# Gate inputs kept two at a time, products by C in a ring of two, and a reordered prologue in a Mamba scan kernel

## What is computed

```
xz = x @ win.T; u, z = split(xz)                  # 1024 channels each
u  = silu(causal_conv4(u) + bconv)
dt, B, C = split(u @ wx.T)                        # 32, 16, 16
delta = softplus(dt @ wdt.T + bdt)
h[n]  = exp(delta * A[n]) * h[n] + delta*u*B[n]   # 16 states a channel, a scan over time
y  = sum_n h[n] * C[n] + u * D
y  = (y * silu(z)) @ wout.T
```

## Time and profile before

| what | us |
|---|---|
| median of the runs | 7417.18 |
| the profiled execution | 7414.95 |
| its span, first to last instruction | 7413.2 |
| PE busy in it | 6753.6 (91%) |
| VectorE busy | 6890.9 (93%) |
| ScalarE busy | 6151.4 (83%) |
| GpSimd busy | 6961.1 (94%) |

### The profile page before, as it was taken

One profiled execution on the slowest core, in us unless ns is written; L12 is line 12 of the kernel. 1 busy time (PEld: TensorE's weight loads), 2 busy tenths in 40 slices (PEclk: granted clock), 3 DMA queues, 4 the chain that ended last, 5 costly groups with the idle time before them and its releaser, 6 DMA issues. The chain is left out here.

```text
span 7413.2 us, 108939 instructions
## 1 busy us (share of the span) xinstructions
PE 6753.6 (91%) x32598; PEld 4030.3 (54%) x32598; DVE 6890.9 (93%) x9252; ACT 6151.4 (83%) x13132; POOL 6961.1 (94%) x3766
## 2 busy tenths in 40 slices
PE   8999999999999998899999899999999999999889
PEld 4555555555555555555555555555555555555455
DVE  6999999999999999999999999999999999999766
ACT  5888888888888888888888888888888888888645
POOL 5999999999999999999999999999999999999678
PEclk9999999999999999999999999999999999999999
DMA  4454444445444444544444454454444544444555
GB/s 163 131 159 138 125 143 140 140 137 157 133 126 141 135 133 128 152 136 116 144 139 133 128 146 140 110 147 138 133 128 143 152 109 144 133 137 129 164 184 171
DMA packets 581024, 1034.51 MB, mean 140 GB/s; under 512 B 100512, under 2 KB 213408, under 8 KB 572256
## 3 DMA queue, kind: packets, MB, share of 16 engines
q1 hardware_dynamic: 576288, 1025.56, 46.6%
q10 hardware_dynamic: 4160, 2.10, 0.1%
HBM read 901.13 MB, written 126.30 MB: 139 GB/s over the span
## 5 line engine op out<-in xcount | busy, mean ns | idle before, releaser
L513 POOL TENSOR_TENSOR dBu<-Bb,du 128x1024 f32<-128x1024 f32 x2048 | 4796.7, 2365 | 2.5 <-DMA Bb<-bc_scratch 2.5
L652 ACT ACTIVATE scans<-delta,A 128x512 f32<-128x512 f32 x4096 | 2744.3, 696 | 233.4 <-DVE hC L1151 223.4
L1135 DVE TENSOR_TENSOR_SCAN scans<-scans,state,dBu 128x512 f32<-128x512 f32 x2016 | 2535.2, 1278 | 226.0 <-ACT scans L652 223.9
L1135 DVE TENSOR_TENSOR_SCAN dBu<-scans,state,dBu 128x512 f32<-128x512 f32 x1568 | 1956.5, 1260 | 7.4 <-ACT scans L652 7.4
L883 PE MATMUL yT<-ident,hC 128*128 128x128 f32 x9216 | 1389.6, 281 | 274.4 <-DVE hC L1151 272.3
L1151 DVE TENSOR_TENSOR hC<-scans,Cb 128x512 f32<-128x512 f32 x2304 | 1553.2, 678 | 2.9 <-PE yT L883 2.8
L525 POOL TENSOR_TENSOR hR<-dBu,Cb 128x512 f32<-128x512 f32 x1024 | 1306.3, 1276 | 216.3 <-DVE dBu L1135 216.0
L883 PEld LDWEIGHTS yT<-ident,hC 128*128 128x128 f32 x9216 | 1077.0, 144 | 568.4 <-DVE hC L1151 345.5
L599 ACT ACTIVATE turned<-bg,CT 128x128 f32<-128x128 f32 x3072 | 877.1, 370 | 246.2 <-PE bg L860 245.6
L876 PE MATMUL bg<-u,comb 128*128 128x512 f32 x2048 | 963.8, 597 | 50.9 <-ACT pre L612 50.0
L834 PE MATMUL bg<-hT,win_z 128*128 128x512 f32 x2048 | 977.7, 600 | 0.0
(11 more groups left out here) (147 smaller groups left out, 7970.2 us busy)
## 6 DMA issues: line engine op xcount, KB each, us to landing
comb<-pre_scratch SPq DMA_DIRECT2D x1024, 256.0 KB, 4.5
Bb<-bc_scratch SPq DMA_DIRECT2D x264, 512.0 KB, 7.0
Cb<-bc_scratch SPq DMA_DIRECT2D x264, 512.0 KB, 7.1
win_u<-in_win SPq DMA_DIRECT2D x264, 256.0 KB, 4.6
win_z<-in_win SPq DMA_DIRECT2D x257, 256.0 KB, 2.7
pre_scratch<-pre SPq DMA_DIRECT2D x256, 256.0 KB, 3.6
comb<-comb_scratch SPq DMA_DIRECT2D x64, 1024.0 KB, 8.2
part_scratch<-pre SPq DMA_DIRECT2D x128, 256.0 KB, 2.0
```

What stands on the lines that cost most here:

```text
L513: pool.tensor_tensor(dBu[:, ring(g, q)], Bb[:, 2 * q:2 * q + 2, :], du[:, j % 2, :].unsqueeze(1).broadcast_to([P, 2, T]), ALU.mult).then_i ...
L652: act.activation(place(n)[:], delta[:, j % 2, :], ACT.Exp, scale=A[:, i // CH_DIR, j * N + n:j * N + n + 1]).then_inc(dA_made, 1)
L1135: nc.vector.tensor_tensor_scan(to, place(n)[:], dBu[:, ring(g, q), k, :], state[:, c:c + 1] if i % CH_SEQ else 0.0, ALU.mult, ALU.add).the ...
```

## The change

- `z` gets two places, `z[:, tile % 2]`. `take_z` then waits only for the gate of the tile before the last one.
- Z1 moves from positions 9, 10 to 4, 5; Z6 from 49, 50 to 45, 46; Z7 from 58, 59 (bank 0) to 50, 51 (bank 1). The visits at p = 15 and 63 go. The one at 7 does the z of tiles 0 and 1, the one at 53 that of tiles 6 and 7 beside the u pair. Z1 is now taken at p = 7, Z6 at 48, Z7 at 53.
- The parts of O0 to O3 are spread anew: O0 (2, 3, 3, 4, 5, 6, 6, 7), O1 8 to 11, O2 12 to 15, O3 16 to 19. O0 is taken at p = 8 where it was 6, O1 at 12 (11), O2 at 16 (15), O3 at 20 as before.
- D7 moves to bank 0, C7 to bank 1, and the late part of the output matrix to p = 53, after Z7 in bank 1.
- The products `hR` get two places where they had four, so GpSimd's product of state 7 waits for TensorE's add of state 3, and that of state 11 for the add of state 4.
- Work for chunks 32 and 33 is left out (`made_in`), with its loads and waits.
- The prologue: `wmod` comes in four pieces, each with a semaphore, and the modulation matmuls loop over k outside. The skip diagonals are made and stored before the first normalization. The stores of `wtap` and the loads of `wgain`, `wproj` and `wout` are issued by ScalarE between its silu steps. `wgain` lies in `Cb[:, 8:12]`.

```diff
-HC, HR = 4, NA
+HC, HR = 4, 2
 GENERAL = [
-    ("D1", (0,), 0), ("Z0", (1, 2), 1), ("O0", (2, 2, 3, 3, 4, 4, 5, 5), 0), ("O1", (6, 6, 7, 7, 9, 9, 10, 10), 0),
-    ("D2", (7,), 1), ("Z1", (9, 10), 1), ("O2", (11, 11, 12, 12, 13, 13, 14, 14), 0), ("D3", (15,), 1),
-    ("O3", (15, 15, 17, 17, 18, 18, 19, 19), 0), ("Z2", (17, 18), 1), ("U0", (20, 20), 1), ("U1", (21, 21), 0),
+    ("D1", (0,), 0), ("Z0", (1, 2), 1), ("O0", (2, 3, 3, 4, 5, 6, 6, 7), 0), ("Z1", (4, 5), 1),
+    ("D2", (7,), 1), ("O1", (8, 8, 9, 9, 10, 10, 11, 11), 0), ("O2", (12, 12, 13, 13, 14, 14, 15, 15), 0), ("D3", (15,), 1),
+    ("O3", (16, 16, 17, 17, 18, 18, 19, 19), 0), ("Z2", (17, 18), 1), ("U0", (20, 20), 1), ("U1", (21, 21), 0),
...
-    ("U7", (43, 43), 1), ("C6", (45,), 0), ("D7", (47,), 1), ("C7", (48,), 0), ("Z6", (49, 50), 1),
-    ("X", (50, 51, 53, 54), 0), ("K", (56,), 1), ("D0", (56,), 0), ("Z7", (58, 59), 0), ("H0", (58,), 1),
+    ("U7", (43, 43), 1), ("C6", (45,), 0), ("Z6", (45, 46), 1), ("D7", (47,), 0), ("C7", (48,), 1), ("Z7", (50, 51), 1),
+    ("X", (50, 51, 53, 54), 0), ("K", (56,), 1), ("D0", (56,), 0), ("H0", (58,), 1),
...
-GATED = {7: (("Z", 0),), 15: (("Z", 1),), 23: (("Z", 2),), 31: (("C", 0), ("Z", 3)), 39: (("C", 2), ("Z", 4)),
-         47: (("C", 4), ("Z", 5)), 53: (("C", 6), ("Z", 6)), 63: (("Z", 7),)}
+GATED = {7: (("Z", 0), ("Z", 1)), 23: (("Z", 2),), 31: (("C", 0), ("Z", 3)), 39: (("C", 2), ("Z", 4)),
+         47: (("C", 4), ("Z", 5)), 53: (("C", 6), ("Z", 6), ("Z", 7))}
...
+def made_in(i, name):
+    if i == 0:
+        return name[0] != "O" and name != f"Y{MT - 1}"
+    if i == CHUNKS - 1:
+        return name[0] not in "UCXKH" and name != "D0"
+    return i < CHUNKS - 2 or name[0] != "H"
...
-        z = sb("z", [P, T])
+        z = sb("z", [P, 2, T])
...
-                                k = ASIDE.index(n)
+                                k = aside(g, n) % HR
                                 pool.wait_ge(h_made, g * N + n + 1 + H0)
                                 pool.wait_ge(hR_used, aside(g, n) + 1)
...
-                act.wait_ge(gated, g + 1)
-                act.copy(z[:], bank[:]).then_inc(bg_free, 1)
+                act.wait_ge(gated, max(tile, 1))
+                act.copy(z[:, tile % 2, :], bank[:]).then_inc(bg_free, 1)
...
             for m in range(RING, MT):
                 sp.wait_ge(bg_ready, PRO_NUM[f"U{m - RING}"] + 1)
                 load_wu(0, m)
-                if m == RING:
-                    sp.dma_start(wproj, io["wprojT"][0:D].rearrange("(k p) n -> p k n", p=P)).then_inc(wout_loaded, 16)
-                    sp.dma_start(wout, io["wout"][0].rearrange("(k p) n -> p k n", p=P)).then_inc(wout_loaded, 16)
```

More of the change, by code:

```diff
@@ L129 @@
 STATS_AT, RSTD_AT, NB_AT = (24, 32, 32, 40), 44, 48
-COMB_AT, COMB_LATE = [3 + 2 * m for m in range(MT)], 52
+COMB_AT, COMB_LATE = [3 + 2 * m for m in range(MT)], 53
 HALF_D = D // 2
-assert COMB_AT[-1] + 1 < AT["U1"][0] and AT["Z6"][-1] < COMB_LATE < AT["K"][0]
+assert COMB_AT[-1] + 1 < AT["U1"][0] and AT["Z7"][-1] < COMB_LATE < AT["K"][0]
 def batch_of_chunk(c):
@@ L229, in scan_stage, with user_of_bank_before @@
         H0, C0, U0, R0, S0, Z0, Y0, DU0 = 2 * AHEAD, HC, HC, HR, 2, 1, 1, 1
+        MADE = [[name for name in BY_END if made_in(i, name)] for i in range(CHUNKS)]
+        TAKEN = [[name for name in BY_ACT if made_in(i, name)] for i in range(CHUNKS)]
+        MADE_TO = [PRO + sum(len(names) for names in MADE[:i]) for i in range(CHUNKS + 1)]
+        TAKEN_TO = [PRO + sum(len(names) for names in TAKEN[:i]) for i in range(CHUNKS + 1)]
+        ALL_READY, ALL_FREED = MADE_TO[CHUNKS], TAKEN_TO[CHUNKS]
         def ready(i, name):
-            if i < 0 or (i == 0 and name in SKIPPED):
-                return PRO
-            return PRO + FIRST_NUM[name] + 1 if i == 0 else (i - 1) * EV + PRO + len(FIRST_NUM) + NUM[name] + 1
+            return MADE_TO[i] + MADE[i].index(name) + 1 if i >= 0 and made_in(i, name) else MADE_TO[max(i, 0)]
         def freed(i, name):
[L239 to L243, removed]
+            return TAKEN_TO[i] + TAKEN[i].index(name) + 1
+        def user_of_bank_before(i, name):
+            users = [other for other, _, bank in SCHEDULE if bank == BANK[name]]
+            at = i * len(users) + users.index(name) - 1
+            while at >= 0 and not made_in(at // len(users), users[at % len(users)]):
+                at -= 1
+            return (at // len(users), users[at % len(users)]) if at >= 0 else (-1, None)
         straight = lambda g, n: g * NS + (len([k for k in STRAIGHT if k < n]) + C0)
@@ L312, in load_BC @@
                             sp.wait_ge(hC_made, straight(last, 2 * q + 2))
+                    if last is None and q == 4:
+                        sp.wait_ge(bg_ready, PRO)
                     src = dram["bc"][s][N + 2 * q:N + 2 * q + 2, :].rearrange("n t -> (n t)")
@@ L315, in load_BC @@
                                  src.partition_broadcast(P)).then_inc(C_loaded[q], 16)
-                    if q == NQ - 3 and last is not None:
+                    if q == NQ - 3 and last is not None and turned is not None:
                         sp.wait_ge(bg_ready, turned)
@@ L429, in _ @@
             sp.wait_ge(bg_free, PRO_NUM["X"] + 1)
[L430 removed]
+            load_BC(0, 16, None, None, 0)
             for i in range(CHUNKS):
@@ L575, in silu_u, with take_z, silu_z @@
                 act.activation(both, both, ACT.Silu).then_inc(u_made, count)
[L577 removed]
+            def take_z(made, bank, tile):
                 act.wait_ge(bg_ready, made)
[L579 to L582 removed]
+                act.wait_ge(gated, max(tile, 1))
+                act.copy(z[:, tile % 2, :], bank[:]).then_inc(bg_free, 1)
+            def silu_z(taken, k):
                 act.wait_ge(bg_free, taken)
[L584 removed]
+                act.activation(z[:, k % 2, :], z[:, k % 2, :], ACT.Silu).then_inc(z_made, 1)
             def take_dbc(made, bank):
@@ L687, in take @@
                 if kind == "Z":
-                    take_z(made, bank, g)
+                    take_z(made, bank, i * MT + k)
             nc.scalar.preload_act_table_set(SILU)
@@ L698, in _ @@
             act.wait_ge(consts_made, 3)
+            act.wait_ge(small_loaded, 48)
+            for d in range(2):
+                for m in range(MT):
+                    ins = act.mul(skip_diag[:, d, m, :], ident[:], skips[:, d, m:m + 1])
+                ins.then_inc(skip_made, 1)
+            act.wait_ge(skip_made, 2)
+            for d in range(2):
+                act.dma_start(dram["skip"][d].rearrange("m p c -> p m c"), skip_diag[:, d]).then_inc(skip_stored, 16)
             deviation(0)
@@ L921, in background @@
                     for piece in range(len(at)):
-                        if at[piece] != p or (i == 0 and name in SKIPPED):
+                        if at[piece] != p or not made_in(i, name):
                             continue
@@ L954, in _ @@
             pe.wait_ge(silu_made, 1)
-            pe.wait_ge(wmod_loaded, 16)
-            for m in range(2 * KD):
-                for k in range(KD):
+            for k in range(KD):
+                pe.wait_ge(wmod_loaded[k], 16)
+                for m in range(2 * KD):
                     ins = nc.tensor.matmul(scans[:, 0, m * NB:(m + 1) * NB], wmod[:, k, m * P:(m + 1) * P], cT[:, k, :],
-                                           start=(k == 0), stop=(k == KD - 1))
+                                           start=(k == 0 and m == 0), stop=(k == KD - 1), skip_group_check=True)
             ins.then_inc(mod_mm, 1)
```

160 lines of the change are left out of this document (72 added, 88 removed).

## The result

The changed kernel takes 7757.18 us, the median of five runs (7751.97 to 7766.56), against 7417.18 for the kernel before. The ratio is 1.0461, 95% interval 1.0449 to 1.0473: slower by 340 us. The forecast said slower by 113 us, with a range that ended at 7590. The direction holds; the size is three times too small.

The account below looks back on a forecast made before the run. No engine alone bounds it: VectorE sets the pace, held up some 7 us a chunk by ScalarE. 7414.95 + 130 (chunks 0 to 29, +4.35 each) - 10 (prologue) - 6 (last chunks) = 7529, given as 7530 us; range 7450 to 7590.

Parts of the forecast that it names:

- ends: Prologue and last chunks: -10 us without the prologue's wait for win_u, -6 us for work left out in chunks 30 and 31.
- the ring's: Product of state 7 waits for the add of state 3, delaying the next tile's first scan: +1.2 us a chunk.
- a part of the stall would be swallowed: Of the ring's 1.8 and 1.4 us, part vanishes where VectorE waits for ScalarE and ScalarE for TensorE; 1.2 left.
- Rival C: Much slower: the ring's stall adds up over all tiles where TensorE is behind, +6.4 us a chunk, 7591; chance 0.14.
- (a): First tiles, p = 4: Z1's weights land late, behind the broadcasts of B and C; TensorE waits 0.9 us.
- (b): First tiles, p = 6: T9 comes one fp32 matmul and the weights' wait later; ScalarE takes it 1.55 us late.
- (c): Visit at p = 7: Z1's copy and a second silu; the scan at p = 8 +2.65 us, its wait becomes 3.6.
- (d): Visit at p = 15 gone: -1.37 us, the scan at p = 16 doesn't wait.
- (e): First tiles: TensorE loses a 1.61 us wait but gains others; net +1.4 us reaches O3, takes at p = 20, later scans.
- (f): p = 45: half of Z6 runs ahead of T89, whose take waits 1.5 us; +0.8 us at p = 48.
- (g): Visit at p = 53: a copy and a silu more, +1.1 us; the scan at p = 54 waits 2.5 us.
- (h): Visit at p = 63 gone: -0.15 us.

Follow-up runs that it names:

- the first four experiments: Two hR places on kernel before: 7662.64; changed kernel with three: 7551.81, with old positions, one z, four hR: 7398.32, with adds of states 3, 4 earlier: 7599.48 us.
- the ring alone: Kernel before with two places for the products hR instead of four, wgain moved to Cb: 7662.64 us against 7413.34.
- the run with the first half alone: Changed kernel with three hR places, the last tiles' pieces and visits put back, the first tiles' left new: 7478.65 us.
- the old schedule: Changed kernel with three hR places and two for z, all moved pieces and eight visits put back as before: 7403.56 us.
- both halves new: Changed kernel with three hR places instead of two, all else as changed: 7551.81 us.
- the run with the ends alone: Changed kernel with old positions and visits, one place for z, four for hR; new prologue and left-out work stay: 7398.32 us.
- The early load: Changed kernel with three hR places, Z1's weights issued before the loads of B and C: 7461.92 us.
- T9's and T89's place: Changed kernel with three hR places, T9 and T89 as TensorE's first work of positions 5 and 45: 7440.80 us.
- ring of two, 7697: Changed kernel, two hR places, Z1's weights issued early, T9 and T89 first in their positions, product of state 7 at q = 6: 7697.27 us.
- ring of three, 7372: Changed kernel with three hR places, Z1's weights issued early, T9 and T89 first in their positions: 7371.71 us.

## Why the prediction was wrong, point by point

Set out by runs, the 344 us between 7413.3 (the kernel before, beside the first four experiments) and 7757.2 are: ends -15, places (three for products, two for z) +5, first tiles +75, last tiles +47, both together another +26, third place to two +205. The forecast had -16, 0, +42, +52, 0 and +36. The runs were made beside several runs of the kernel before (7412.7 to 7421.8 us), so each term is good to some 5 us.

**The step that failed is the ring's.** The wait itself was foreseen: the product of state 7 waits for the add of state 3, 7.0 us in tile 2 by my sum and 4.56 in the trace after. Then I asked only for the next tile's first scan, ten microseconds of GpSimd's work further on, and said that in six of eight tiles the sum stayed below what VectorE had anyway. The nearer consumer was left out. Behind the product in GpSimd's queue stand `delta`, `du` and the `dBu` of step 7 of the same tile, and its consumer is that tile's own scan: 2214.66 - 2208.48 = 6.2 us from the product's start to that `dBu`'s end, and rows 8 give the product (1.26) and a `dBu` (9.33 for four) the same lengths in the kernel before. The add of state 3 in tile 2 was over at 2110.99 and in tile 4 at 2165.06 (rows 8); with 0.2 to be seen and these 6.2 us the scans of step 7 could not start before 2117.4 and 2171.5. They had started at

```profile
2114.57 2.46 DVE L1135 TENSOR_TENSOR_SCAN scans<-scans,state,dBu 128x512 f32<-128x512 f32 x2
...
2168.60 2.46 DVE L1135 TENSOR_TENSOR_SCAN scans<-scans,state,dBu 128x512 f32<-128x512 f32 x2
```

in the kernel before. The differences are 2.8 and 2.9 us; the ring alone made gaps of 2.9 and 3.0 there. The row was there to be read. In tiles 0, 1, 3 and 5, where I had the ring cost nothing, the ring alone made gaps of 1.1 to 1.8 us at the same step. So the ring costs 7.8 us a chunk on the kernel before (223.4 for 215.6 on the mean) and 6.9 on the changed one beside three places (227.0 for 220.1), and not my 1.2 or its upper bound, 3.2. The statement that would have shown it, "with VectorE waiting for dBu at the starts of tiles 3 and 5", came out the other way: it waits at the ends of tiles 2 and 4.

**A second error stood beside it**: that a part of the stall would be swallowed. Some is, about a third, where a scan used to wait behind a visit; I had counted on nearly two thirds. And the upper bound of a chunk, 5.5 us with nothing absorbed, isn't the sum of its terms: 1.4 + 3.2 + 1.75 is 6.35, and with the terms' own upper bounds it is 8.2. That would have put the top at some 7645, still 112 us short, as step 7 stood in none of them.

**Rival C** had the right idea, that the stall isn't swallowed, but took it from tiles 2 and 4 alone. It gave 7591.

**First tiles, +75 for +42.** (a) Z1's weights do land late, as forecast, and where forecast: in the run with the first half alone 15.8 us behind the first scan on the mean, 15.8 named (16.0 in the changed kernel). But TensorE waits for them 1.66 us a chunk in that run, not 0.9, for it gets there earlier than I had it. (b) ScalarE takes T9 at 22.2 us of a chunk there (22.3 in the changed kernel). In the kernel before the mean is 19.6; chunk 9, from which I read it, has 20.1. So T9 is 2.6 us late and not 1.55: 0.75 from the wait and some 0.4 from one chunk taken for all. This 1.1 us a chunk is of the size of the missing 33 us. (c) The scans at p = 7 and 8 wait 2.43 and 1.98 us, 4.4 together, where 3.6 were named for p = 8 alone. With the old schedule the two waits are 0.5 together, so they grew by 3.9 and not by the 2.65 of the sum: short by about that 1.1 again. (d) Right: no gap at p = 16. (e) TensorE's lateness shows at p = 21, where the gap goes from 1.64 to 2.09, less than the +1.4 that I had it carry that far.

**Last tiles, +47 for +52.** (f) Right in its own terms: the wait of the T89 take is 1.51 us where 1.5 was named. (g) Right: the gap at p = 54 is 2.71 for 2.5 named. (h) Right in sign; the gap at the next chunk's start (0.15 in the old schedule) is below 0.1.

**Table loads and ends.** 192 of each for 256, at the same 1283 ns, and the next activation starts 1.29 us behind the start of the load (2158.12 and 2159.41 in the timeline of the visit): the drain of which the Trainium skill speaks (ScalarE: Activation LUTs, What ACT_TABLE_LOAD costs) doesn't show here either, nor ahead of the load, which starts 0.02 us behind the end of z's copy. The loads' busy time fell by the 164 us of the trace's price; ScalarE as a whole gained 150 by the new schedule (6119.7 with both halves old, 5969.3 with both new). Prologue and last chunks gave 15 us for 16, a sum that is right partly by luck: in the run with the ends alone the first scan comes 8.3 us earlier for the 10 named and chunk 31 is 6.1 us shorter for 5, but chunks 0 to 30 take 7 us less, which wasn't named, and the stretch behind the last scan 2 us more (19 us in the two profiled executions, 15 by the medians).

**What stays open.** Why both halves together cost 26 us more than the sum of the two wasn't looked into. The early load gave 2.9 us a chunk and T9's and T89's place 3.6, more than T9's 2.4 or 2.5 us each; where the rest comes from isn't shown. The mean granted clock is 0.962 in the changed kernel and 0.976 before; in the experiments it goes with the waits, 0.961 (ring of two, 7697) and 0.973 (ring of three, 7372). The stretches at the lower of its two levels (1.2 and not 2.4 GHz) add up to 590 us in the changed kernel and 362 before, and in them records of `yT<-ident,hC` in a row stand 213 ns apart and not 109. So the 228 us more of slow clock can have cost TensorE some 114 us of its own work at most, an estimate from these rows; how much of that lies on VectorE's path, and so within the ring's price, isn't shown.

## What to carry to other kernels

When a wait is added to an engine that works through a queue in order, write down everything queued behind it up to the next wait and check each against its own consumer, the nearest first: the price is set by the first consumer without slack, not by the first one that comes to mind. A smaller ring is cheap where the waiting operation stands behind the urgent work and dear where it stands ahead of it: here the same ring of two costs 326 us or 16, by one step of one product. And before a switch of tables is merged with another, get the work that stands ahead of it (weights, a transposition) there in time; the schedule with the merged visits lost 148 us without that and stood some 30 ahead of the old one with it, of which the old one, not run with the same two moves, may win a part too.

## What had not been expected

- Issuing one 256 KB load ahead of sixteen 512 KB broadcasts, rather than behind them, was worth 90 us (2.9 a chunk). Its landing behind the chunk's first scan went with the time at which the last tile's products had been added, through SyncE's waits: 16.0 us in the changed kernel, 18.6 with one add a position later.
- Moving four 128x128 records ahead of four to six of 128x512 within one position of TensorE, twice a chunk, gave 111 us, and moving adds ahead in the same manner cost 56 where nobody waited for them.
